# A decoder's first stage: its first layer norm folded into the query weights and into the second norm's epsilon

## What is computed

```
def _layernorm(x, axis=-1, eps=1e-05):
    m = jnp.mean(x, axis=axis, keepdims=True)
    v = jnp.var(x, axis=axis, keepdims=True)
    return (x - m) / jnp.sqrt(v + eps)
...
    qh = _xpos(q @ Wq, offset=0, inverse_scale=False)
    kh = _xpos(k @ Wk, offset=0, inverse_scale=True)
    vh = v @ Wv
...
    scores = jnp.einsum('bld,bmd->blm', qh, kh) * mask[None, :, :]
    return scores @ vh
...
    x = _layernorm(x + _L0_attn_ref(x, L0_attn_a_param, ...), axis=-1)
    x = _layernorm(x + _L0_xattn_ref(x, ctx_1024, ctx_1024, L0_xattn_Wq, L0_xattn_Wk, L0_xattn_Wv), axis=-1)
    x = _layernorm(x + _L0_ffn_ref(x, ...), axis=-1)
```

## Time and profile before

| quantity | value |
|---|---|
| runs | 1636.11, 1639.2, 1642.05 us; median 1639.2 |
| span of the profiled execution | 1630.7 us (the median of the runs less 8.5) |
| TensorE busy | 1492.4 us, 92% |
| VectorE busy | 1125.7 us, 69% |
| ScalarE busy | 820.4 us, 50% |
| GpSimd busy | 602.4 us, 37% |
| stage A, in the profiled execution | to 261.9 us, where routing begins |

### The profile page before, as it was taken

How to read it: one execution, slowest core, us unless ns; L and a number is a source line. 1 busy time by engine, 2 the same in 40 slices (tenths; PEclk the granted TensorE clock), 3 DMA queues, 4 the chain that set the end, 5 groups by cost and what they waited for, 6 DMA issues and landing times.

```text
span 1630.7 us, 34497 instructions
## 1 busy us (share of the span) xinstructions
PE 1492.4 (92%) x12742; PEld 1336.6 (82%) x12742; DVE 1125.7 (69%) x2334; ACT 820.4 (50%) x1559; POOL 602.4 (37%) x700
## 2 busy tenths in 40 slices
PE   4888888899999999978888789999979999979997
PEld 3777777799999999866777668888879999979997
DVE  3899987756555655318888548888866776757684
ACT  6777742245544544425666536656524444434442
POOL 3666651212122211037777302313214444433444
PEclk8999999899999999989999979999989999999999
DMA  6222253203233321062332142222136455463543
GB/s 192 66 78 77 71 192 111 91 27 104 91 104 103 100 94 40 14 226 65 89 94 75 65 165 66 68 80 80 35 74 127 93 108 118 83 125 76 107 87 73
DMA packets 118159, 152.11 MB, mean 93 GB/s; under 512 B 10090, under 2 KB 102852, under 8 KB 117508
## 3 DMA queue, kind: packets, MB, share of 16 engines
q1 hardware_dynamic: 110068, 127.48, 28.4%
q0 software_dynamic: 6560, 19.02, 4.1%
q10 hardware_dynamic: 1392, 3.70, 0.6%
HBM read 111.37 MB, written 38.80 MB: 92 GB/s over the span
## 4 chain that ended last, share of the span: by engine, by line
PE 35%; issue 6%; DVE 5%; DMA 4%; ACT 3%; POOL 3%; SPq 1%; DVEq 0%; POOLq 0%; ACTq 0%
PE psum L531 14%; PE psum L1875 4%; PE psum L498 3%; PE psum L506 3%; DMA arena_x<-wT_d 2%; PE psum L1852 2%; PE psum L1449 2%; PE psum L1843 2%; DVE psum L2460 1%; PE psum L1830 1%; PE psum L1837 1%; POOL arena_y L1425 1%; PE psum L490 1%; DMA wT_d<-arena_w 1%; ACT arena_y L1549 1%
## 5 line engine op out<-in xcount | busy, mean ns | idle before, releaser
L2231 POOL TENSOR_TENSOR d_g_parts<-arena_w,d_g_parts 128x512 fp32r<-128x512 f32 x128 | 166.3, 1299 | 246.3 <-ACT d_g_parts L2363 242.3
L531 PE MATMUL psum<-d_v_high,d_g_parts 128*128 128x256 f32 x1024 | 206.4, 285 | 3.1 <-DVE arena_x L2001 2.3
L531 PE MATMUL psum<-d_x_parts,d_v_high 128*128 128x256 f32 x1024 | 194.4, 287 | 9.4 <-issue 8.0
L531 PE MATMUL psum<-m_w_high,m_h_parts 128*128 128x256 f32 x1024 | 188.0, 284 | 0.0
L1213 ACT ACTIVATE arena_x<-psum,b_e 128x512 f32<-128x512 f32 x128 | 88.2, 689 | 189.8 <-PE psum L531 87.4
L1141 POOL DMA_INDIRECT arena_x<-x_d,slot_row x64 | 67.9, 1062 | 292.4 <-PE psum L1187 228.2
L531 PEld LDWEIGHTS psum<-d_x_parts,d_v_high 128*128 128x128 f32 x1024 | 159.8, 192 | 16.4 <-issue 10.6
L531 PEld LDWEIGHTS psum<-d_v_high,d_g_parts 128*128 128x128 f32 x1024 | 169.3, 192 | 3.9 <-issue 3.1
L531 PE MATMUL psum<-m_xF_parts,m_w_high 128*128 128x512 f32 x512 | 159.7, 393 | 2.1 <-DVE m_xF_parts L526 2.1
L531 PEld LDWEIGHTS psum<-m_w_high,m_h_parts 128*128 128x128 f32 x1024 | 160.7, 192 | 0.0
L2371 ACT ACTIVATE arena_y<-psum 128x512 f32<-128x512 f32 x128 | 76.2, 595 | 155.9 <-PE psum L531 155.9
(11 more groups left out here) (281 smaller groups left out, 3737.9 us busy)
## 6 DMA issues: line engine op xcount, KB each, us to landing
arena_x<-wT_d SPq DMA_DIRECT2D x128, 256.0 KB
arena_y<-in_L_ffn_w SPq DMA_DIRECT2D x16, 1024.0 KB, 7.9
x_d<-arena_x SPq DMA_DIRECT2D x32, 256.0 KB, 2.2
y_d<-arena_x SPq DMA_DIRECT2D x16, 512.0 KB, 8.9
arena_x<-kv_d SPq DMA_DIRECT2D x16, 512.0 KB, 3.5
kv_d<-arena_x SPq DMA_DIRECT2D x9, 512.0 KB, 2.9
arena_x<-in_x SPq DMA_DIRECT2D x16, 256.0 KB, 2.9
arena_x<-in_ctx SPq DMA_DIRECT2D x16, 256.0 KB, 3.0
```

The costliest lines, as they stand in the source:

```text
L531: ins = nc.tensor.matmul(dst, left[a_], right[b_], start=start and k == 0, stop=stop and k == 2, skip_group_check=True)
L2231: nc.gpsimd.tensor_tensor(K["gP"][:, s % 4, 1], K["g"][:, s % 2], K["gP"][:, s % 4, 0].bitcast(F32), ALU.subtract).then_inc(d_gl, 1)
```

## The change

Layer norm 1 is no longer applied. With r1 the residual, m its mean, v its variance and s = sqrt(v + eps), x1 is (r1 - m)/s. The attention is linear in its query, so (r1 - m) Wq gives s times the result; and r1 Wc, where Wc is Wq less the mean of each of its columns, is (r1 - m) Wq. So r2 = r1 + result is s times the old r2, plus m. Layer norm 2 takes m out, and its epsilon must be s squared times eps: (v + eps) * eps. In the code:

- Wq is centred once, in step 3: TensorE multiplies a matrix of ones with Wq (two matmuls into bank 4), VectorE subtracts (one instruction, in place).
- Queries are projected from r1 itself, so this projection stands at position 3, in the step in which r1 is transposed; keys, values and context move forward one position with it. The whole pipeline has `A_LAG` = 5.
- ScalarE copies the transposed r1 out as `rT` (in the place of the copy to x1F). VectorE takes the statistics of norm 1 from rT a position later, at the head of the step; they yield only (v + eps) * eps, in `A_eps`.
- The application of norm 1 (two VectorE instructions a step), its power on GpSimd (one) and the transposition of x1 (four on TensorE) are gone. The last statistics instruction of norm 2 becomes an addition of two SBUF operands, variance and A_eps.
- GpSimd's write of r1 also waits for the query projection of two units before. The loads of context and the stores of context and x2 are issued a step earlier.

Cut to its core:

```
-        A_LAG = 6
+        A_LAG = 5
...
+                if t.fixed and t.n == 3:
+                    pe.wait_ge(s_weights, 16 * len(weights_in))
+                    pe.wait_ge(s_tables, 16)
+                    for c in range(NC_):
+                        ins = nc.tensor.matmul(bank(4)[:, 0:D], table("ones"), w["L0_xattn_Wq"][:, c, :],
+                                               start=(c == 0), stop=(c == NC_ - 1))
+                    ins.then_inc(a_sum, 1)
...
-                if u4:
-                    done(pe, a_x1F, u4)
-                    done(pe, a_qp, u4.back(1), 2)
-                    project(bank(4), "L0_xattn_Wq", A["x1F"][:, u4.p], par=True).then_inc(a_q, 1)
+                if u3:
+                    if t.fixed and t.n == 3:
+                        pe.wait_ge(a_centred, 1)
+                    done(pe, a_qp, u3.back(1), 2)
+                    project(bank(4), "L0_xattn_Wq", A["r1"][:, u3.p], par=True).then_inc(a_q, 1)
...
-                if u3:
-                    done(pe, a_x1, u3)
-                    to_feature(bank(1), A["x1"][:, u3.p]).then_inc(aT_x1, 1)
...
                 if u3:
-                    done(act, aT_x1, u3)
-                    done(act, a_q, u3.back(2))
-                    nc.scalar.activation(A["x1F"][:, u3.p], chunks(bank(1)), ACT.Copy).then_inc(a_x1F, 1)
+                    done(act, aT_r1, u3)
+                    done(act, a_r2, u3.back(2))
+                    nc.scalar.activation(A["rT"][:, u3.p], seqs(bank(1)), ACT.Copy).then_inc(a_rT, 1)
...
-                if u3:
-                    done(dve, aT_r1, u3)
-                    ln_stats(dve, u3, seqs(bank(1)), A_st1, ln1)
+                if u4:
+                    done(dve, a_rT, u4)
+                    ln_bn(dve, u4, A["rT"][:, u4.p], A_st1, ln1)
+                    ln_moments(dve, u4, A_st1, ln1)
+                    done(dve, ln1[0], u4, 2)
+                    nc.vector.tensor_scalar(A_eps[:, :, :], A_st1[:, :, 7:8], LN_EPS, LN_EPS, ALU.add,
+                                            ALU.mult).then_inc(ln1[1], 1)
+                if t.fixed and t.n == 3:
+                    dve.wait_ge(a_sum, 1)
+                    nc.vector.scalar_tensor_tensor(w["L0_xattn_Wq"][:, :, :],
+                                                   bank(4)[:, None, 0:D].broadcast_to([P, NC_, D]), -1.0 / D,
+                                                   w["L0_xattn_Wq"][:, :, :], ALU.mult, ALU.add).then_inc(a_centred, 1)
...
-                if u3:
-                    done(dve, aT_x1, u3.back(2))
-                    done(dve, a_r2, u3.back(2))
-                    ln_apply(dve, u3, seqs(bank(1)), A["x1"][:, u3.p], A_st1, ln1)
-                if u5:
-                    done(dve, a_r2, u5)
-                    ln_stats(dve, u5, A["r2"], A_st2, ln2)
...
+                    done(dve, a_r2, u4)
+                    ln_bn(dve, u4, A["r2"], A_st2, ln2)
+                    ln_moments(dve, u4, A_st2, ln2)
+                    done(dve, ln2[0], u4, 2)
+                    done(dve, ln1[1], u4)
+                    nc.vector.tensor_tensor(A_st2[:, :, 9:10], A_st2[:, :, 7:8], A_eps[:, :, :],
+                                            ALU.add).then_inc(ln2[1], 1)
...
-                if u3:
-                    rstd(pool, u3, A_st1, ln1)
...
+                    done(pool, a_q, u2.back(2))
```

More of the change, by code:

```diff
@@ L453, in ln_moments @@
         def ln_moments(dve, u, stats, sems, cell=0):
-            s_st, s_ag, s_rs, s_out = sems
+            s_st = sems[0]
             dve.wait_ge(s_st, u.n * 2 + 1)
@@ L547, in decoder @@
             A[n] = arena_x.take([P, 2, UB, D])
-        for n in ("xF", "cF", "thx", "tha", "a", "inv", "m", "g", "h", "r1", "x1F", "kr", "x2F"):
+        for n in ("xF", "cF", "thx", "tha", "a", "inv", "m", "g", "h", "r1", "kr", "x2F"):
             A[n] = arena_x.take([P, 2, NC_, T])
@@ L553, in decoder @@
             A[n] = arena_x.take([P, NC_, T])
-        for n in ("x1", "x2", "v"):
+        for n in ("rT", "v", "x2"):
             A[n] = arena_x.take([P, 2, UB, D])
@@ L559, in decoder @@
         A_st1 = sb("A_st1", [P, UB, 10])
+        A_eps = sb("A_eps", [P, UB, 1])
         A_st2 = sb("A_st2", [P, UB, 10])
         a_in, a_inc, a_cst = sem2("a_in"), sem2("a_inc"), sem2("a_cst")
-        aT_x, aT_c, aT_r1, aT_x1, aT_x2 = (sem("aT_" + n) for n in ("x", "c", "r1", "x1", "x2"))
+        aT_x, aT_c, aT_r1, aT_x2 = (sem("aT_" + n) for n in ("x", "c", "r1", "x2"))
+        a_sum, a_centred = sem("a_sum"), sem("a_centred")
         a_gate, a_k, a_v, a_q, a_score, a_ret, a_logit = (
             sem("a_" + n) for n in ("gate", "k", "v", "q", "score", "ret", "logit"))
-        a_xF, a_cF, a_thx, a_tha, a_dec, a_vs, a_x1F, a_x2F, a_lg = (
-            sem("a_" + n) for n in ("xF", "cF", "thx", "tha", "dec", "vs", "x1F", "x2F", "lg"))
+        a_xF, a_cF, a_thx, a_tha, a_dec, a_vs, a_rT, a_x2F, a_lg = (
+            sem("a_" + n) for n in ("xF", "cF", "thx", "tha", "dec", "vs", "rT", "x2F", "lg"))
         a_init, a_inv, a_min, a_cap, a_sq, a_rt, a_g1, a_u, a_r, a_mg, a_xe, a_h, a_r1 = (
@@ L619, in step @@
             def step(t):
-                u0, u1, u3, u4, u5, u6 = (t.at(k, UNITS) for k in (0, 1, 3, 4, 5, 6))
+                u0, u1, u2, u3, u4, u5 = (t.at(k, UNITS) for k in range(6))
                 if u3:
                     done(pe, a_r1, u3)
-                    done(pe, a_x1F, u3.back(1))
+                    done(pe, a_rT, u3.back(1))
                     for b in range(UB):
@@ L650, in step @@
                     ins.then_inc(a_gate, 1)
+                if u3:
+                    done(pe, a_cF, u3)
+                    done(pe, a_kt, u3.back(1), 2)
+                    project(bank(5), "L0_xattn_Wk", A["cF"][:, u3.p], par=True).then_inc(a_k, 1)
                 if u4:
-                    if t.fixed and t.n == 4:
-                        pe.wait_ge(s_weights, 16 * len(weights_in))
-                    done(pe, a_cF, u4)
-                    done(pe, a_kt, u4.back(1), 2)
-                    project(bank(5), "L0_xattn_Wk", A["cF"][:, u4.p], par=True).then_inc(a_k, 1)
@@ L657, in step @@
-                if u5:
-                    done(pe, a_sc, u5)
-                    done(pe, a_vs, u5)
-                    for b in range(UB):
-                        ins = nc.tensor.matmul(bank(6)[:, b * D:(b + 1) * D], A["sc"][:, u5.p, b, :],
-                                               A["v"][:, u5.p, b, :], start=True, stop=True)
-                    ins.then_inc(a_ret, 1)
-                if u4:
-                    done(pe, a_x1F, u4)
-                    done(pe, a_qp, u4.back(1), 2)
-                    project(bank(4), "L0_xattn_Wq", A["x1F"][:, u4.p], par=True).then_inc(a_q, 1)
@@ L668, in step @@
[L668 to L678 removed]
+                    done(pe, a_sc, u4)
@@ new lines, in step @@
+                    done(pe, a_vs, u4)
+                    for b in range(UB):
+                        ins = nc.tensor.matmul(bank(6)[:, b * D:(b + 1) * D], A["sc"][:, u4.p, b, :],
+                                               A["v"][:, u4.p, b, :], start=True, stop=True)
+                    ins.then_inc(a_ret, 1)
+                if u3:
+                    if t.fixed and t.n == 3:
+                        pe.wait_ge(a_centred, 1)
+                    done(pe, a_qp, u3.back(1), 2)
+                    project(bank(4), "L0_xattn_Wq", A["r1"][:, u3.p], par=True).then_inc(a_q, 1)
@@ L679, in step @@
+                if u5:
+                    done(pe, a_x2, u5)
+                    done(pe, a_x2F, u5.back(1))
+                    to_feature(bank(0), A["x2"][:, u5.p]).then_inc(aT_x2, 1)
+                    done(pe, a_x2F, u5)
+                    if u4:
+                        done(pe, a_sc, u4)
                     for b in range(UB):
@@ L713, in step @@
             def step(t):
-                u0, u1, u2, u3, u4, u6 = (t.at(k, UNITS) for k in (0, 1, 2, 3, 4, 6))
+                u0, u1, u2, u3, u5 = (t.at(k, UNITS) for k in (0, 1, 2, 3, 5))
                 if u2:
@@ L861, in step @@
             def step(t):
-                u2, u3, u4, u5 = (t.at(k, UNITS) for k in (2, 3, 4, 5))
-                if u3:
-                    rstd(pool, u3, A_st1, ln1)
+                u2, u3, u4 = (t.at(k, UNITS) for k in (2, 3, 4))
                 if u2:
```

141 lines of the change are left out of this document (67 added, 74 removed).

## The result

| quantity | before | after |
|---|---|---|
| median of the runs | 1639.4 us (1636.1 to 1642.1) | 1626.9 us (1624.1 to 1628.7) |
| ratio after/before | | 0.9927, interval 0.991 to 0.9945 |
| span of the profiled execution | 1630.7 us | 1626.9 us |
| last copy of logits ends (end of stage A) | 261.94 us | 249.11 us |
| mean of steps 6 to 16 | 13.70 us | 12.84 us |

The forecast was 1625.4 us, with the last copy of logits at 248.0 (a start; measured 248.93). The sum came out right by luck: the ten middle steps were 2.4 us shorter than forecast, steps 4 to 6 were 3.0 us longer, and the picture of the steady step behind the forecast was not what the trace shows. One further execution of the kernel after, in its second measurement, took 2151.11 us at a granted clock of 0.646 and is left out of every number here.

A forecast was written before the change was run, and what follows sets the result against it. Bound: a loop through all four engines, with VectorE's L810 held by GpSimd's L871. Stage A: 30.14 + 12.5 + 170.7 + 14.2 + 9.8 + 10.66 = 248.0 against 261.76, gain 13.8; span 1616.9, time 1625.4 us, range 1617 to 1632.

The forecast's parts named there:

- rival B: Stage A's steady steps: L810 sometimes beats L871, steps of 12.4 and 13.13 in turn, gain 18.1, time 1621.1 us; 22%.
- The period: Stage A's full step: falls from 13.64 by 0.51 to 13.13 us, L810 still starting behind L871.
- T + 11.7: VectorE's arrival at L810, counted from the decay's start T: about 0.5 us earlier than T + 12.21, still later than L871.
- the stated range: Whole kernel's time: 1617 to 1632 us, holding the forecast, B and half of D.
- TensorE's term: TensorE from x2's transposition to the logits, each steady step: 1.80 us becomes 1.29, shortening the loop by 0.51.
- Filling: Stage A's start: step 3 takes 12.5 us, then steps 4 to 16 all count as steady, 13 by 13.13 = 170.7.
- bound on step 3: New step 3, with centring: longer than 11.44 and shorter than 13.64 us, taken as 12.5.
- rival E: Stage A's steady steps: TensorE's waits grow and its clock falls, 1.65 us a step, time 1646.9 us; 4%.
- Draining: Stage A's end: step 17 14.2, new step 18 9.8, then 10.66 us; old step 18, about 10 us, has no successor.
- C: Stage A's steady steps: TensorE sets all of them at 12.4 us, gain 23.3, time 1615.9 us; 5%.
- D: Stage A's steady steps: a new collision, for instance at L849, keeps the period 13.64; gain 7.1, time 1632.1 us; 14%.
- 8.5 us: Whole kernel: the run median's excess over the profiled span, added to the forecast span 1616.9 to give 1625.4 us.

The follow-up runs named there:

- first two experiments: Against the kernel after: r1's statistics moved behind the decay product, 1620.1 us; separately, two idle VectorE instructions from PSUM added, 1631.4 us in one execution.
- third experiment: Four transpositions (of r1, without a new wait) put back on TensorE between x2's transposition and the logits, against the kernel after: 1619.8 us in one execution.
- sixth experiment: Centring of the query weights moved from step 3 into steps 1 and 2, against the kernel after: 1623.6 us, ratio 0.9908.
- the last: Gates ahead of scores in steps 4 and 5 alone, against the kernel with five edits (1619.2 us): 1615.8 us, ratio 0.986.
- fourth experiment: Addition L849 of two SBUF tensors replaced by two tensor_scalar instructions with one SBUF input each, against the kernel after: 1619.4 us in one execution.

## Why the prediction came out right, and where it was wrong

**The sum**, in us of stage A:

| stretch | before | forecast | rival B | after |
|---|---|---|---|---|
| start of step 3 | 30.14 | 30.14 | 30.14 | 31.31 |
| step 3 | 11.44 | 12.5 | 12.5 | 11.61 |
| steps 4 to 6 | 38.78 | 39.4 | 38.4 | 42.35 |
| steps 7 to 16 | 136.40 | 131.3 | 128.0 | 128.92 |
| from step 17 to the end of A | 45.2 | 34.7 | 34.7 | 34.9 |

(B's 12.8 a step is taken for all thirteen.) Before and after differ by 12.8 us, of which 10.3 come from the drain and 7.5 from the ten steady steps; 1.3 and 3.6 were given back up to step 6. Of the 1.3, 1.2 is the later start of step 3, which differs between executions. (The forecast counted to the start of the last copy, 0.18 us before its end.) Against the forecast, 2.4 us too many in steps 7 to 16 stand against 3.0 too few in steps 4 to 6. Neither was foreseen, so that their sum fits is luck; the drain is the part that was right for the reason given.

**The period: the failing step is VectorE's arrival.** I took T + 11.7 for L810's successor out of T + 11.2 to 11.7, since GpSimd's chain would hold VectorE back. Measured, from the decay's start 129.48, L823 starts at T + 11.18: all of the 1.00 us came through. GpSimd's rotation ended at T + 7.78 instead of T + 8.55, 0.77 earlier, more than the 0.68 of idle time that I allowed less a stretch; the other quarter came between the applied norm 2 and the maximum, where the statistics now follow at once. L883 was at T + 11.60, near the forecast's 11.49. So L823 wins by 0.42, and the step is rival B's: 12.36, where B had 12.4. The other step is 13.37, not 13.13. Strict turns would give 12.87; the mean of steps 6 to 16 is 12.84. B's reason for the alternation, that the second scan waits for L871's successor, is not what happened: L837 has no wait, and it is the keys that VectorE waits 0.91 for. That steps of two lengths, as in rival B, were the case and the port their cause is shown by the first two experiments. So the mechanism that the forecast named, L810 at 1.6 us in every step, was wrong, and the time alone would not have shown it: B's 1621.1 and the forecast's 1625.4 both lie within the stated range.

**TensorE's term.** From the transposition of x2 to the logits it is 1.37 us (132.64 to 134.01) against the 1.29 taken from the drain: the gain was 0.43 instead of 0.51, with the new wait at 0.77 instead of 0.69. The transpositions in it were worth nothing by themselves (third experiment).

**Filling.** The bound on step 3 held, 11.61 against 12.5. What I held for free was step 4, counted as a steady one. With a step less, the first scores stand in step 4 right behind the rotation of their queries: GpSimd's L907 ended at 46.20 (44.96 and 1.24), while TensorE was ready at 43.5. The centring's wait of 2.30 in step 3 did not make it later: without it TensorE's wait was 2.72 again. The clock, whose price I had put to rival E in the steady steps, was paid here, 0.71 and 1.10 in two rows. Steps 4 and 5 took 30.0 instead of 26.3, and that is what hid the error in the period. The sixth experiment took 1.7 us out of step 4, all of it clock, and the last 3.1, of which 1.3 was clock.

**Draining.** Step 17 took 14.41 (forecast 14.2), step 18 9.67 (9.8), and from there to the start of the last copy 10.66 (10.66). The wait of step 17 is 2.35 where before had 2.41, and the lower clock behind it is in both lengths; in the fourth experiment, where the clock did not fall there, the step took 12.72. The 10 us of the old step 18 are the surest part of the gain; no experiment puts that step back, and the reading rests on the rows.

**The other rivals.** C is out, since TensorE sets only every second step. D is out, yet one thing that it named is true: L849 is held by GpSimd, 0.37 against 0.16, where I wrote that no row shows so small an instruction held, and the Trainium skill's rule (SBUF — State Buffer, "Who interferes with whom") does hold for it. It just costs little: without it the period fell by 0.12. E is out: TensorE's waits in a long step, 0.77 and 0.77, are hardly longer than 0.72 and 0.71, the short step has only the second, its rows there have their short durations, and the granted clock from 70 to 190 us was 1.00.

**From the span to the runs.** I added 8.5 us to the span as what lies around it. In the profiled execution of the kernel after it is 1628.7 less 1626.9, 1.8 us. The rest of the 8.5 was that the profiled execution of before had a short part behind stage A, 1368.8 us where the eleven profiles of the kernel after and its variants have 1370.7 to 1377.8. The number was right for carrying a median, and its name wrong. (Carried at 1.8 us, the median of before would have asked for 1375.7 us behind stage A and that of after for 1376.0: no difference.)

## What to carry to other kernels

Where two engines race for one resource, ask not only how long the loser waits but who arrives first and by how much. If a change moves one of them by more than the gap, compute both orders and look for an alternation, since the one that loses in this step often wins the next. Price the first steps of a pipeline by themselves when a step is taken out of it, since work that had a whole step of slack in the full pipeline may stand behind its producer at the start.

## What the hardware showed that I had not expected

- Very small VectorE instructions are held until the GpSimd instruction beside them ends, as large ones are. A tensor_scalar of 128x2 in fp32 from one SBUF input took 0.95 us beside GpSimd's L889 and 0.16 to 0.17 elsewhere, and a tensor_tensor of 128x2 took 0.37 beside L899 and 0.16 with GpSimd idle. The Trainium skill (SBUF — State Buffer, "Who interferes with whom") counts tensor_scalar among the instructions that can take the port pair shared with GpSimd. The trace agrees, down to 256 elements.
- One or two waits of up to 0.79 us in each steady step left TensorE's rows at their short durations (the eight matmuls of L617 at 1.89). Behind the wait of 2.35 in step 17 the same eight took 3.54 (granted clock 0.65 from 222 to 225 us), and behind that of 2.72 in step 4 the gates took 2.99: by these durations most of both ran at the lower level. The length of the wait alone does not decide it: with the early centring the gates behind the same 2.72 us took 1.89, and with the two small instructions (fourth experiment) the eight matmuls behind the same 2.35 us took 1.89.
- The 1370 us behind stage A, the same instructions in all kernels, took from 1368.8 to 1377.8 us in the profiled executions. A gain of 5 us in one stage can't be read from two spans.
